# Embedding-interaction kernel: another order of turns, gather holds and layer parts

## What is computed

```
h = relu(dense @ dw1 + db1)                      # 512 x 13 -> 64
dense_emb = relu(h @ dw2 + db2)                  # 512 x 64
sparse_emb = emb_tables[f_ids, sparse_idx]       # 512 x 26 x 64, one row of a table for each field
emb = concatenate([dense_emb[:, None, :], sparse_emb], axis=1)    # 512 x 27 x 64
inter = einsum('bfd,bgd->bfg', emb, emb)         # 27 x 27 dot products for each sample
pairs = inter[:, iu0, iu1]                       # the 351 above the diagonal
z = concatenate([emb.reshape(512, -1), pairs], axis=1)
z = relu(z @ ow1 + ob1)                          # 2079 -> 512
z = relu(z @ ow2 + ob2)                          # -> 256
z = relu(z @ ow3 + ob3)                          # -> 128
return z @ ow4 + ob4                             # -> 1
```

## Time and profile before

| | us |
|---|---|
| median of 3 runs (lowest to highest) | 188.17 (187.83 to 189.74) |
| the profiled execution, own time | 187.21 |
| its span, first to last instruction | 185.4 |
| mean granted clock of TensorE in it | 0.88 |
| PE busy | 127.4 (69%) |
| POOL busy | 123.8 (67%) |

### The profile page before, as it was taken

How to read it: one execution, slowest core, us unless ns; L and a number is a source line. 1 busy time by engine, 2 the same in 40 slices (tenths; PEclk the granted TensorE clock), 3 DMA queues, 4 the chain that set the end, 5 groups by cost and what they waited for, 6 DMA issues and landing times.

```text
span 185.4 us, 3069 instructions
## 1 busy us (share of the span) xinstructions
PE 127.4 (69%) x1301; PEld 68.8 (37%) x1301; DVE 37.8 (20%) x97; ACT 42.2 (23%) x96; POOL 123.8 (67%) x199
## 2 busy tenths in 40 slices
PE   1510285828655995839439993959729979989994
PEld 0000132514344442524226432424426446656453
DVE  2700003000142204100144005000234023136011
ACT  0440310031046201040075001040174011166011
POOL 3888888888735888888565888888367887200000
PEclk9999999975965699996965798587997999999999
DMA  5999532221212332312312332222222324100000
GB/s 157 409 332 357 172 26 23 23 28 21 21 13 23 21 22 24 28 22 26 24 13 24 23 27 20 23 28 20 19 20 20 22 25 31 18 4 0 4 0 0
DMA packets 4576, 9.80 MB, mean 53 GB/s; under 512 B 2065, under 2 KB 2065, under 8 KB 3922
## 3 DMA queue, kind: packets, MB, share of 16 engines
q0 software_dynamic: 3328, 3.41, 21.3%
q1 hardware_dynamic: 1010, 5.30, 7.1%
q10 hardware_dynamic: 224, 0.89, 1.6%
HBM read 9.59 MB, written 0.00 MB: 52 GB/s over the span
## 4 chain that ended last, share of the span: by engine, by line
PE 45%; POOL 26%; issue 18%; ACT 5%; DMA 3%; DVE 2%
PE acc L259 20%; POOL gathered L211 20%; PE acc L292 10%; PE inter L276 7%; POOL pace L219 6%; PE acc L310 4%; DMA gathered<-tables,rows 2%; ACT emb L386 1%; ACT emb L387 1%; PE turned L240 1%; PE acc L301 1%; ACT pairs L392 1%; DMA idx_raw<-idx 1%; ACT z L399 1%; DVE emb L466 1%
## 5 line engine op out<-in xcount | busy, mean ns | idle before, releaser
L211 POOL DMA_INDIRECT gathered<-tables,rows x104 | 98.9, 951 | 34.6 <-issue 16.9
L259 PE MATMUL acc<-w,emb 128*128 128x512 f32 x104 | 65.7, 780 | 19.4 <-issue 12.3
L259 PEld LDWEIGHTS acc<-w,emb 128*128 128x128 f32 x104 | 31.3, 315 | 46.3 <-issue 36.9
L392 ACT ACTIVATE pairs<-inter 28x96 f32<-28x96 f32 (+1 forms) x64 | 15.7, 246 | 39.8 <-PE inter L276 39.1
L219 POOL MEMSET pace<- 128x192 uint8 x90 | 24.7, 274 | 0.1
L292 PE MATMUL acc<-w,pairs 128*128 128x512 f32 x56 | 24.7, 592 | 0.0
L182 DVE COPY pairs<-inter 28x96 f32<-28x96 f32 (+1 forms) x64 | 17.0, 266 | 26.5 <-PE inter L276 25.8
L276 PE MATMUL inter<-emb 64*28 64x28 f32 x1024 | 12.6, 204 | 13.8 <-DMA gathered<-tables,rows 10.1
L240 PE MATMUL turned<-small,gathered 128*128 128x128 f32 x52 | 10.1, 317 | 13.5 <-DMA gathered<-tables,rows 13.5
L386 ACT ACTIVATE emb<-turned 128x512 f32<-128x512 f32 x8 | 8.8, 1098 | 45.7 <-issue 28.6
L465 DVE COPY emb<-turned 128x512 f32<-128x512 f32 (+1 forms) x7 | 5.5, 784 | 64.1 <-issue 49.5
(11 more groups left out here) (47 smaller groups left out, 26.3 us busy)
## 6 DMA issues: line engine op xcount, KB each, us to landing
w<-w SPq DMA_DIRECT2D x5, 1024.0 KB, 8.7
gathered<-tables,rows POOLq DMA_INDIRECT x104, 3.4
small<-small_pack ACTq DMA_DIRECT2D x1, 706.5 KB, 6.0
dense_sb<-dense_pack ACTq DMA_DIRECT2D x1, 160.5 KB
idx_raw<-idx SPq DMA_DIRECT2D x1, 39.0 KB
idx_raw<-idx SPq DMA_DIRECT2D x1, 13.0 KB, 1.9
out<-y SPq DMA_DIRECT2D x1, 2.0 KB
```

The source lines that it names most:

```text
L211: pool.indirect_dma_start(out=gathered[:, t, s, :], out_offset=None, in_=tables, in_offset=bass.IndirectOffsetOnAxis(ap=rows[:, t, s:s + 1 ...
L259: nc.tensor.matmul(acc[t][:], emb[:, tile_of(t), place(2 * c)], w[:, c, :], start=(c == 0), stop=False)
L392: last = move(lambda dst, src: nc.scalar.activation(dst, src, ACT.Copy), t, k, (0, 1))
```

## The change

- The last tile has five groups, (0,4), (4,8), (8,10), (10,12), (12,13), in place of four; the helpers take their bounds from `groups(t)`.
- In tiles 0 to 2, group 3 is turned directly behind group 2, ahead of the products of group 2. The products of group 3 stand between the two halves of the interactions; both halves now stand ahead of the turn of group 0 of the next tile, and the pair product ahead of the products of group 0.
- The held gathers are numbers 4 and 7 (the 5th and the 8th).
- The pace write is 256 bytes, and it is left out behind gathers 0 to 7 of tile 0, 8 to 15 of the other tiles, and as before 18 to 25 of the last one: 58 writes in place of 90.
- Layers 2 to 4 run in three parts: samples 0 to 255 (in tile 2), 256 to 383 (in tile 3) and 384 to 511 (at the end).
- ACT moves both halves of the interactions before it keeps group 0.

```
+LAST_GROUPS = [(0, 4), (4, 8), (8, 10), (10, 12), (12, 13)]
...
-EARLY = LAST * P
-PACE = 192
-HOLDS = [7, 10]
-UNPACED_FROM = 18
+PARTS = [slice(0, 2 * P), slice(2 * P, 3 * P), slice(3 * P, B)]
+PACE = 256
+HOLDS = [4, 7]
+UNPACED = [range(0, 8), range(8, 16), range(8, 16), [*range(8, 16), *range(18, NF)]]
...
+def groups(t):
+    return LAST_GROUPS if t == LAST else GROUPS
...
-            sp.wait_ge(y_done, 2)
+            sp.wait_ge(y_done, len(PARTS))
...
-                        elif t < LAST or s < UNPACED_FROM:
+                        elif s not in UNPACED[t]:
                             nc.gpsimd.memset(pace[:, t * NF + s, :], 0)
...
             for t in range(TILES):
                 if t:
                     interactions(t - 1, 0)
+                    field_products(t - 1, 3)
+                    interactions(t - 1, 1)
                 turn(t, 0)
                 if t:
-                    interactions(t - 1, 1)
+                    pair_product(t - 1)
                 field_products(t, 0)
                 if t:
-                    pair_product(t - 1)
                     z1_to_features(t - 1, at_once)
                 turn(t, 1)
-                if t < LAST:
+                if t == LAST:
+                    break
+                if t == LAST - 1:
+                    layer2(PARTS[0], 1, whole, (acc[0], acc[1]))
+                    field_products(t, 1, 0, 2)
+                    layer3(PARTS[0], 0, acc[3])
+                    field_products(t, 1, 2)
+                    layer4(PARTS[0], 0, acc[0])
+                else:
                     field_products(t, 1)
-                    turn(t, 2)
-                    field_products(t, 2)
-                    turn(t, 3)
-                    field_products(t, 3)
-
-            layer2(early, LAST - 1, [[(m, k) for m in range(2) for k in range(K1)]], (acc[0], acc[1]))
-            c0, c1 = GROUPS[1]
-            field_products(LAST, 1, (c0, c0 + 1))
-            layer3(early, 0, acc[2])
-            field_products(LAST, 1, (c0 + 1, c0 + 3))
+                turn(t, 2)
+                turn(t, 3)
+                field_products(t, 2)
+
+            layer2(PARTS[1], 2, whole, (acc[1], acc[2]))
+            field_products(LAST, 1, 0, 2)
+            layer3(PARTS[1], 1, acc[1])
             turn(LAST, 2)
-            layer4(early, 0, acc[0])
-            field_products(LAST, 1, (c0 + 3, c1))
+            field_products(LAST, 1, 2)
+            layer4(PARTS[1], 1, acc[2])
+            field_products(LAST, 2)
             turn(LAST, 3)
-            c0, c1 = GROUPS[2]
+            field_products(LAST, 3, 0, 1)
+            turn(LAST, 4)
             interactions(LAST, 0)
-            field_products(LAST, 2, (c0, c0 + 2))
+            field_products(LAST, 3, 1)
+            field_products(LAST, 4)
             interactions(LAST, 1)
-            field_products(LAST, 2, (c0 + 2, c1))
-            field_products(LAST, 3)
             pair_product(LAST)
             z1_to_features(LAST, Z1_STEPS)
-            layer2(late, LAST, LAYER2_STEPS, (acc[1], acc[2]))
+            pe.wait_ge(y_done, 2)
+            layer2(PARTS[2], LAST, LAYER2_STEPS, (acc[1], acc[2]))
...
             for t in range(TILES):
                 if t:
                     moves(t - 1, 0)
+                    moves(t - 1, 1)
                 keep(t, 0)
                 if t:
-                    moves(t - 1, 1)
                     z1_relu(t - 1, at_once)
+                if t == LAST - 1:
+                    z2_relu(PARTS[0], 0, acc[0])
+                    z3_relu(PARTS[0], 0, acc[3])
                 if t == LAST:
-                    z2_relu(early, 0, acc[0])
-                    z3_relu(early, 0, acc[2])
+                    z2_relu(PARTS[1], 1, acc[1])
+                    z3_relu(PARTS[1], 1, acc[1])
                 keep(t, 2)
```

More of the change, by code:

```diff
@@ L124, in build @@
         ones_set = sem("ones_set")
-        group_in = [[sem(f"group_in{t}_{g}") for g in range(NG)] for t in range(TILES)]
+        group_in = [[sem(f"group_in{t}_{g}") for g in range(len(groups(t)))] for t in range(TILES)]
         gathers_held = sem("gathers_held")
@@ L207, in _ @@
                     pool.wait_ge(rows_done, 1)
-                for g, (c0, c1) in enumerate(GROUPS):
+                for g, (c0, c1) in enumerate(groups(t)):
                     for s in range(2 * c0, 2 * c1):
@@ L248, in kept, with field_products @@
             def kept(t, g):
[L250 to L254, removed]
+                if g % 2 or g == NG:
+                    pe.wait_ge(kept_dve, t * 2 + g // 2 + 1)
+                if g % 2 == 0:
+                    pe.wait_ge(kept_act, t * 2 + g // 2 + 1)
+            def field_products(t, g, first=0, end=W_GROUP):
                 if t == 0:
@@ L257, in field_products @@
                 kept(t, g)
-                for c in range(*(chunks or GROUPS[g])):
+                c0, c1 = groups(t)[g]
+                for c in range(c0 + first, min(c0 + end, c1)):
                     nc.tensor.matmul(acc[t][:], emb[:, tile_of(t), place(2 * c)], w[:, c, :],
@@ L266, in interactions @@
                         pe.wait_ge(dense_placed, 1)
-                    kept(t, 2)
-                    kept(t, 3)
+                    for g in range(2, len(groups(t))):
+                        kept(t, g)
                     if t:
@@ L326, in layer4 @@
                 nc.tensor.matmul(bank[0:1, 0:n], ow4, z3t[:, samples], start=True, stop=True).then_inc(y_mm, 1)
-            early, late = slice(0, EARLY), slice(EARLY, B)
             at_once = [(0, K1)]
+            whole = [[(m, k) for m in range(2) for k in range(K1)]]
             for t in range(TILES):
@@ L435, in _ @@
             z1_relu(LAST, Z1_STEPS)
-            z2_relu(late, 1, acc[1])
-            z3_relu(late, 1, turned[1])
+            z2_relu(PARTS[2], 2, acc[1])
+            z3_relu(PARTS[2], 2, turned[1])
         @block.vector
@@ L499, in _ @@
                 keep(t, 1)
+                if t == LAST - 1:
+                    z2_relu(PARTS[0], 0, acc[1])
+                    outputs(PARTS[0], 0, acc[0])
                 if t == LAST:
-                    z2_relu(early, 0, acc[1])
-                    outputs(early, 0, acc[0])
-                if t < LAST:
-                    keep(t, 3)
-            dve.wait_ge(group_turned, TILES * NG)
-            nc.vector.tensor_copy(evens(LAST, NG - 1), turned_all(NG - 1)).then_inc(kept_dve, 1)
+                    z2_relu(PARTS[1], 1, acc[2])
+                    outputs(PARTS[1], 1, acc[2])
+                keep(t, 3)
+            dve.wait_ge(group_turned, LAST * NG + NG + 1)
+            nc.vector.tensor_copy(evens(LAST, NG), turned_all(LAST, NG)).then_inc(kept_dve, 1)
             moves(LAST, 0)
@@ L509, in _ @@
             z1_features(LAST, Z1_STEPS)
-            z2_relu(late, 1, acc[2])
-            outputs(late, 1, inter[0])
+            z2_relu(PARTS[2], 2, acc[2])
+            outputs(PARTS[2], 2, inter[0])
 def lay_out(inputs):
```

38 lines of the change are left out of this document (18 added, 20 removed).

## The result

The changed kernel took 203.01 us (median of four runs, 202.29 to 203.36), the kernel before 188.89 beside it (four runs, 187.83 to 189.74): a ratio of 1.0746, with an interval of 1.067 to 1.082. The forecast was 184.9. The profiled execution had 203.36 with a span of 201.5 and a mean granted clock of 0.863.

What follows compares the result with a forecast made beforehand. Bound: a chain through POOL's gathers up to tile 3's second hold, then PE. Interactions ending about 4.9 us earlier, less what waits behind them, gave a span of 182.2 against 185.4, in proportion 184.9 us; range 181.2 to 188.8.

Steps and rivals of the forecast that it cites:

- Part 2: Holds and turns: a first hold loses 0.8 us, a tile takes 39.9 against 40.1; tile 3's gather 8 starts at 134.9.
- Part 3: Layers in three parts: 4.9 us of PE work in tile 2 costs nothing, 3.4 us leave tile 3's path.
- Part 1: Pace writes on POOL: 256 bytes make a gather step 1.44 us (bounds 1.39 and 1.48); an unpaced gather saves 0.14.
- the wait of 2.25: Last tile: moving the second half of the interactions takes 2.25 us with nothing beside it, before the last pair product.
- Stops inside the interactions: Pauses inside a half of the interactions: 1.1 us in one row, none in the other; 0.5 added to the span.
- part 4: Last tile from 134.6: pair product first, 6.1 us plus 1.5 for the low clock; last pair product at 168.7, end 181.7.
- D: Rival, chance 0.14: group 2's products (-0.8 each, tiles 1 to 3) and the pair product (-1.5) at full clock: 181.6 us.
- B: Rival, chance 0.13: PE bounds every tile, the pair product behind the interactions at low clock throughout; span 192.1, 195.0 us.
- C: Rival, chance 0.16: no difference; interactions stop in their middle in each hold, six halves by 1.1 us; median 188.8.
- E: Rival, chance 0.07: gathers without a write follow no faster than with one, costing 3.4 us in all: 188.4.
- What would show it: List of signs: right, steps of 1.44 and 1.25 and tiles near 40; wrong, first hold over 4.5 us in every tile.
- The rule weighed in the prediction: PE's short bursts between waits start slow every round; so the new order is no cure, its result being B.

Runs made afterwards that it cites:

- the kernel with 192 bytes: The changed kernel with pace writes of 192 bytes in place of 256, left out at the same places: 184.14 us on chip 6, 212.12 on chip 10.
- the two variants of it on chips 6 and 9: The kernel before with only the new writes (256 bytes, eight left out per tile), 184.60 us on chip 6; and with no write at all, 175.71 on chip 9.

## Why the prediction was wrong

**The failed step** is in parts 2 and 3: "So it costs nothing while the low clock adds less than 2 us there", and with it the costing at nothing of every turn, relu and keep that the new order puts into the stretch of unbroken gathers. Each of those terms took it that a signal of PE arrives as its last matmul ends, as ahead of 42.37, where the turn and a keep of 2.38 follow each other. On the chip of the result they came 2 to 8 us late there. Layers 2 to 4 are a chain of such signals, PE to ACT and DVE and back. The kernel before goes through it with its 384 samples once; the change twice inside the gathers of tiles 2 and 3.

**The sum, term by term** (forecast of span 182.2, measured 201.5, 19.3 more):

- To gather 8 of tile 2: 95.38 for 95.0. Part 1 was right: a step with a write takes 1.44 (65.43 to 66.87), one without 1.25 (55.42 to 56.67), a write 0.33. Of part 2 the first hold was nearly right in tiles 1 and 2: from the start of gather 25 to that of gather 5 it took 11.5 and 11.0 (forecast 11.0).
- To gather 8 of tile 3: 6.2 late, of which 5.9 arose in this tile. Layer 2 took 3.72 (forecast 3.7). The turn of group 2 starts 12.9 behind the transposes at 109.25, in the kernel with 192 bytes 9.9 behind its own at 106.45: 3.0. The keep of group 2 is later by another 2.6 (125.44 - 122.17 less 117.02 - 116.33). Then the eight products took 6.19 for my 5.3. That is 6.5, a little of which fell into slack. (By the 3.4 of the earlier trace rows gather 23, issued at 115.50, landed at 118.9, an estimate; the turn of group 2 started 3.3 later.)
- From there to the last pair product: 45.5 for 33.8, 11.7 more. Moves and pair product took 2.4 and 7.78 (forecast 2.25 and 7.6), the products of group 0 3.60, layer 2 was over 3.6 behind them (3.7). From the end of layer 2 at 158.13 to the end of the turn at 173.64 it took 15.5 in place of 6.8: 8.7 more, 6.4 of it in the waits 1.60, 3.85 and 0.98 and the rest in layer 3, a turn and products behind them, mostly at the low clock (2.93 for 1.8; the granted clock was 0.64 from 168.1 to 171.1). The last 2.8 are mostly four products between the interactions, 3.79 in place of 1.9; these are no late signal, the kernel with 192 bytes on chip 6 has the same 3.79, and the granted clock was 0.50 from 178.85 to 182.7.
- The end: 14.8 in place of 13.0. The pair product took 7.94 and not 6.1. The windows of the kernel after have its granted clock as 0.78 (the column ahead of the last two):

```profile
186.70:194.60 7.90, 7.90 (x14) 3.12 (x14) 0.00 (x0) 0.00 (x0) 0.00 (x0) 0.78 0.00 0
```

In before it was 1.00 from 172.4 to 178.5, where six field products ran first. The prediction charged the wait of 2.25 but left the pair product at "as today". That is a term mis-sized by 1.8, apart from the failed step; the kernel with 192 bytes shows it too. It isn't fixed by the order: behind the same wait of 2.42 the new order with the old writes took 6.25 on chip 6, and so did the change itself on chip 10.
- Stops inside the interactions: 0.5 forecast for tile 3, and there were none; tile 1 had 0.26 and 0.49.

6.2 + 11.7 + 1.8 - 0.5 is 19.2.

**Where there are no late signals** the part that runs through POOL came no later than forecast, and the last tile still missed. The kernel with 192 bytes starts gather 8 of tile 3 at 131.81, 3.1 ahead of the forecast for the change, whose writes are longer. From there it takes 52.9 to the end of its span (184.7), where the forecast has 46.8: 6.1 more without a late signal. Most of it is the clock: 9.00 for the pair product of tile 2 (7.6), 3.79 for the four products (1.9), 7.94 for the last (6.1). That 169.81 for its last pair product lies near the forecast 168.7 is luck, two misses that nearly cancel. The trace is of its slowest execution, 186.51.

**Slips in the recorded sums.** The write of 0.10 us is of one number of four bytes and not of one byte, which moves the step by less than 0.01. Part 3's terms add up to 116.2 and not 116.5, with a pair product of 6.1 where part 4 takes 7.6 for the same kind (8.47 came, and used up the slack). D's terms give 178.3 and not 178.9. None of these is the failure.

**The rivals.** B's time, 192.1 in span, lies nearest, but not by its mechanism: the pair product took 7.78 to 8.47 straight behind the interactions, not 12.2. In tile 2 that is 2.4 over the 6.1 counted there, just past the 2 us from which B was to decide. C's stops came once. E was wrong: gathers without a write followed at 1.25. D's full clock came for the products of group 2 in tile 1 alone (3.82). "What would show it" did name the signs: a first hold of over 4.5 (9.75 from gather to gather, though in tile 3 alone), a pair product of over 8 (8.47), a turn of group 2 behind gather 23's landing (122.17), a pair product of tile 3 behind 171 (186.68). No rival held a signal between engines that is late for longer: none of the rows that the prediction rests on has one, and the 18% "in which nothing is waited for" were not followed up. The trace of before does have a small one. PE's timeline first, then ACT's:

```profile
159.08 0.81 PE L320 MATMUL acc<-z2t,small 128*128 128x384 f32 x2
```

```profile
160.64 0.58 ACT L408 ACTIVATE z3t<-acc,small 128x384 f32<-128x384 f32 x1 [4.86 <-PE acc L320]
```

Layer 3 is over at 159.89 and ACT, idle, starts its relu 0.75 later; in the kernel before on chip 8 it is 0.42, in the two variants of it on chips 6 and 9 0.03 to 0.04. The kernel before is also about 1 to 2% shorter on chips 6 and 9 than on the others. The warning was there, but nothing in its size told of 8 us.

The rule weighed in the prediction (the Trainium skill, TensorE: Matmul & The Clock Gate, "HAM oscillation — how this bites in real kernels") fared better than my sum at the end of this kernel: the burst behind the wait had a granted clock of 0.78 where I had the full clock. The trace agrees, for 1.8 us of the 19.3. It isn't so in every round: behind the same wait the same burst took 6.25 in the two runs named above, and the granted clock of the new order with the old writes was 1.00 from 167 to 177.

## What to carry to other kernels

When work that hops from engine to engine (matmul, relu, matmul, relu) is to be moved beside a stream of back-to-back indirect gathers, compare the end of each producer with the start of its consumer, on more than one chip: a dependency that costs 0.04 us on one cost up to 14.65 on another. A pause that looks like pure cost on the issuing engine, here a write that nobody reads, can be what lets others through: taking it out gave 5.1% on one chip and cost 12.9% on another. And a change is judged on the chips where it will run: by chip 6 alone a neighbour of this one would have passed as no loss (0.4% under before), while it costs 13.5% on chip 10.

## What the runs showed of the hardware that I had not expected

- While POOL issues indirect gathers one behind another, or shortly behind them, PE's semaphore updates for ACT and DVE can be late: by 1.5 to 8 us in the kernel after, up to 13.3 (chip 8) and 14.65 (chip 10) without the writes. On chips 6 and 9 none was late, the four of these programs that also ran on chips with late signals included. The profile books such a wait as "another core or an unknown queue", as "issue", or as PE's (115.35). Several late starts of the kernel after lie about 2.9 us apart, two steps of a gather (112.44, 115.35, 118.26, 121.12, 124.00), and on chips 8 and 10 they do so too; in the kernel after each of these five falls within 0.03 of the end of a write, on chip 8 up to 0.34 ahead of it.
- The length of the pause counts: on chip 10 199.2 us with 256 bytes, 212.1 with 192, 223.7 with none. No pause of another kind was run.
- Gathers land within 3.2 to 3.7 us of their start in the kernel before, and on chip 8 too, but within 2.3 to 7.5 in the kernel before without writes on chip 9 and 2.4 to 7.5 in the one with 192 bytes on chip 6. No one program has this figure on both kinds of chip, so whether chip or program makes the difference is open, as is what ties it to the signals.
- PE's clock behind the same wait isn't the same each time: the last pair product took 6.25 in three kernels of the new order (one of them the change on chip 10) and 7.94 in most others, each behind 2.4 us of idle PE.
